# A gated cross-attention and expert block on one core: first-norm statistics moved to ScalarE, products that nobody reads, tile 1 transposed on TensorE, the first weight units split in pieces

## Chip, core and metric

The kernel runs on one core of a Trainium2 chip. The time is device microseconds of one execution. A profiled execution gives the trace; its span runs from the first to the last instruction.

## What is computed

Eight sequences of 256 tokens (2048 tokens, width 256) pass a cross-attention over 64 sets and then a block of 8 experts, of which each token takes two:

```python
def layernorm(x): return (x - mean(x)) / sqrt(var(x) + 1e-5)

# attention: token_states = layernorm(x), set_states = ctx (8, 64, 256)
q = token_states @ W_q.T + b_q
scores = (q @ desc_router.T) / 16                 # 64 sets
scores = where(set is one of the token's 4, scores, -inf)
weights = softmax(the 2 best scores)              # others 0
x = x + tanh(g_xattn) * (weights @ set_states)

# experts: xf = layernorm(x)
logits = xf @ gate_w + gate_b                     # 8 experts
top 2 logits, softmax over them; comb = gate_score * alpha
y = sum over e of comb[e] * (gelu(xf @ fc1_w[e] + fc1_b[e]) @ fc2_w[e] + fc2_b[e])
x = x + tanh(g_ffn) * y
```

## The kernel before

It is written engine by engine, with semaphores by hand; the order of the calls in each engine's block is the order of its work.

**The front, up to about 73 us.** The 16 token tiles of 128 go in four groups (g = 0 to 3) of four tiles (GT). Per group:

- `transpose_pair` (TensorE) transposes x in two pairs of tiles into banks 0 and 1, `copy_pair` (ScalarE) copies them out, `score_pair` (TensorE) multiplies by `rhs_c`, whose 73 columns are 64 projected set scores, 8 gate columns and the negative mean. `keep_gate` (ScalarE) keeps the last nine columns in `xgate`.
- `norm1` (VectorE) computes the variance of x with bn_stats and bn_aggr (four of each) and one tensor_scalar; `rsqrt` (GpSimd) makes `rs1` of it.
- `pick_sets` (VectorE) scales and masks the scores (`pick_scores`, line 982), takes the top two and marks them; `set_exp` (ScalarE) takes the exponentials; `weigh_sets` (VectorE, line 1012) makes the weights; `transpose_weights` (TensorE) and `copy_weights` (ScalarE) turn them round; `attention` (TensorE) multiplies with the sets. It needs `ctxgw` for group 0: `transpose_sets`, `copy_sets`, `set_gates` and one copy (line 822).
- `add_attention` (VectorE, from line 1020) adds the result to x; `squares` (ScalarE) and `variance2` (VectorE, line 1042) give the second variance; `route` picks two experts; `ranks` (TensorE, lines 496 to 500) counts the picks ahead of each token; `slots` (VectorE) makes places of them; `normalise` (ScalarE) and `row_low` (VectorE) write the normalised rows as two f16 parts, which SyncE stores in DRAM (`xrows`).

`projection` of the sets (line 520, read by VectorE at line 959) and the mask (lines 962 to 972) come ahead of group 0's scores. In VectorE's block `norm1(0)` stands ahead of line 959, `norm1(1)` behind the mask, `norm1(2)` and `norm1(3)` behind `pick_sets(0)` and `pick_sets(1)`.

**Into the second part, 73 to 84 us.** `token_table` sums one-hot products into a table of the tokens of each expert; from it comes `fetch_at`, with which GpSimd gathers the rows of the first four tiles (`fetch_rows`). Tile 0 is transposed by TensorE (line 589) and copied by ScalarE (line 866), tile 1 and all later ones by a transposing DMA of SyncE (line 412). The weights of 16 units (fc1 and fc2 of 8 experts, 2048 f32 columns each) lie in SBUF; a unit is split into two f16 parts by `weights_hi` (ScalarE, line 806) and `weights_lo` (VectorE, line 1297).

**The second part.** 39 tiles of 128 picks. Tile i runs fc1 in eight chunks of six products (line 615), with fc2 of the two tiles before between them (three products a chunk, line 631, 256 columns). Between stand gelu (ScalarE, line 877) and the split of its result (VectorE, lines 1432 and 1434).

## Time and profile before

| | us |
|---|---|
| median of the runs before | 307.38 (306.29 to 309.16, 3 runs) |
| span of the profiled execution | 304.3 |
| TensorE busy | 251.6 (83%) |
| VectorE busy | 213.1 (70%) |
| ScalarE busy | 177.5 (58%) |
| GpSimd busy | 147.2 (48%) |

The page's slices are 40 equal parts of the span (7.6 us each), a digit is the busy share or the granted clock in tenths. A timeline row is a start, the time to the last end, engine, line, operation and count; a bracket gives the idle time before it and what ended it. A chain row is a piece of the chain of work that ended last.

### The profile page before, as it was taken

To read this page: it belongs to the slowest core of one execution; us is meant where nothing else is said; L and a number is where in the kernel's file an instruction comes from. 1 tells how busy PE (TensorE), PEld (TensorE's weight loads), DVE (VectorE), ACT (ScalarE), POOL (GpSimd) and SP (SyncE) were. 2 spreads that over 40 slices of the span, in tenths; PEclk is the share of its full clock that TensorE was granted. 3 is DMA by queue.
4 is the path that set the end of the run, shared out by engine and by line. 5 is a ranking of instruction groups with operands and counts; after the bars stand their busy time and mean duration, and the time that the engine had idled before them with its cause. 6 is when DMAs were issued, how large, how long until landed. Compare 5 with 4: busy or idle time off the path is not lost.

```text
span 304.3 us, 9126 instructions
## 1 busy us (share of the span) xinstructions
PE 251.6 (83%) x3075; PEld 235.6 (77%) x3075; DVE 213.1 (70%) x701; ACT 177.5 (58%) x491; POOL 147.2 (48%) x122
## 2 busy tenths in 40 slices
PE   2999534241799999999999999999999999999910
PEld 2998433231689989999999999999999999989900
DVE  4899999896789778686677768677866555455500
ACT  2144878776574766856766685676666545555400
POOL 2121148994524556677545464454536355444240
PEclk9999855555599999999999999999999999999995
DMA  6999999996414444474534454455454536452320
GB/s 179 336 375 377 378 371 378 377 322 214 106 34 77 73 72 70 73 83 80 97 63 74 88 74 80 80 77 69 77 84 74 87 55 94 69 77 32 37 31 3
DMA packets 47262, 41.06 MB, mean 135 GB/s; under 512 B 23569, under 2 KB 43794, under 8 KB 47090
## 3 DMA queue, kind: packets, MB, share of 16 engines
q1 hardware_dynamic: 39088, 29.75, 33.0%
q0 software_dynamic: 7488, 10.39, 23.1%
q8 instruction: 28, 0.46, 0.6%
q10 hardware_dynamic: 642, 0.33, 0.4%
q14 instruction: 16, 0.13, 0.1%
HBM read 26.10 MB, written 9.37 MB: 117 GB/s over the span
## 4 chain that ended last, share of the span: by engine, by line
PE 60%; DVE 12%; DMA 6%; issue 3%; ACT 3%; POOL 1%; DVEq 0%; POOLq 0%; ACTq 0%
PE bank L615 30%; PE bank L631 29%; DMA out_dram<-xn,add_at 4%; DMA xs<-xrows,fetch_at 1%; DVE rows L1052 1%; DVE wreg L1061 1%; DMA xTp<-xs 1%; ACT wreg L806 1%; ACT rows L877 1%; DVE xs L1031 1%; DVE earlier L1105 1%; DVE wreg L1297 1%; DVE gmark L1095 1%; POOL out_dram L1529 1%; POOL xs L1521 1%
## 5 line engine op out<-in xcount | busy, mean ns | idle before, releaser
L615 PE MATMUL bank<-xTp,wreg 128*128 128x128 f16 x1872 | 155.3, 221 | 1.4 <-ACT xTp L866 0.7
L631 PE MATMUL bank<-wreg,rows 128*128 x936 | 150.5, 273 | 0.3 <-DVE rows L1434 0.3
L615 PEld LDWEIGHTS bank<-xTp,wreg 128*128 x1872 | 131.1, 99 | 9.6 <-issue 1.4
L877 ACT ACTIVATE rows<-bank,maskbias 128x128 f32<-128x128 f32 x312 | 88.9, 371 | 42.1 <-PE bank L615 21.6
L1529 POOL DMA_INDIRECT out_dram<-xn,add_at x39 | 66.7, 1711 | 88.1 <-DMA out_dram<-xn,add_at 48.8
L631 PEld LDWEIGHTS bank<-wreg,rows 128*128 128x128 f16 x936 | 79.1, 98 | 4.3 <-issue 0.4
L1432 DVE TENSOR_SCALAR rows<-rows 128x512 f16<-128x512 f32 x78 | 36.5, 468 | 41.6 <-ACT rows L877 41.5
L1521 POOL DMA_INDIRECT xs<-xrows,fetch_at x39 | 47.1, 1206 | 23.2 <-issue 11.3
L1434 DVE SCALAR_TENSOR_TENSOR rows<-rows 128x512 f16<-128x512 f32 x78 | 54.0, 693 | 2.7
L1297 DVE SCALAR_TENSOR_TENSOR wreg<-wreg (+1 forms) x16 | 36.7, 2292 | 13.9 <-ACT wreg L806 13.3
L885 ACT ACTIVATE xn<-xn,maskbias 128x256 f32<-128x256 f32 x39 | 20.0, 513 | 36.9 <-DVE xn L1423 36.8
L806 ACT ACTIVATE wreg<-wreg (+1 forms) x16 | 30.7, 1919 | 2.0 <-DVE wreg L1297 1.6
L1487 POOL TENSOR_TENSOR rs<-ve,neg_half 128x4 f32<-128x4 f32 x8 | 8.3, 1036 | 32.7 <-DVE ve L913 19.9
L1423 DVE SCALAR_TENSOR_TENSOR xn<-bank,xs 128x256 f32<-128x256 f32 x39 | 16.3, 418 | 7.3 <-PE bank L631 7.0
L1495 POOL TENSOR_SCALAR at_col<-iota,place_f,token 128x128 f16<-128x128 f32 x12 | 12.2, 1028 | 0.0
L498 PE MATMUL bank<-picks,before 128*128 128x32 f32 x8 | 2.5, 405 | 11.4 <-DVE earlier L1105 11.4
L498 PEld LDWEIGHTS bank<-picks,before 128*128 128x128 f32 x8 | 2.0, 316 | 11.7 <-DVE earlier L1105 7.9
L437 PE MATMUL bank<-rhs_c,xTp 128*128 128x73 f32 x64 | 10.9, 326 | 0.1
L424 PE MATMUL bank<-ident,xs 128*128 128x128 f32 x32 | 6.3, 347 | 5.5 <-DMA xs<-in_x_dram 5.5
L437 PEld LDWEIGHTS bank<-rhs_c,xTp 128*128 128x128 f32 x64 | 10.2, 242 | 0.5 <-issue 0.3
L712 ACT ACTIVATE xTp<-bank 128x512 f32<-128x512 f32 x8 | 4.7, 596 | 9.4 <-PE bank L424 9.3
L1495 POOL TENSOR_SCALAR wreg<-iota,place_f,token 128x128 f16<-128x128 f32 x8 | 8.2, 1037 | 2.7 <-DVE place_f L1153 2.7
(202 smaller groups left out, 208.0 us busy)
## 6 DMA issues: line engine op xcount, KB each, us to landing
wreg<-in_L_ffn_fc_w_dram SPq DMA_DIRECT2D x16, 1024.0 KB, 12.7
xrows<-rows SPq DMA_DIRECT2D x4, 528.0 KB, 6.4
xs<-in_x_dram SPq DMA_DIRECT2D x4, 512.0 KB, 9.3
out_dram<-xs SPq DMA_DIRECT2D x4, 512.0 KB, 9.1
xs<-in_L_ffn_fc_b_dram SPq DMA_DIRECT2D x1, 1024.0 KB, 5.7
xs<-xrows,fetch_at POOLq DMA_INDIRECT x39
out_dram<-xn,add_at POOLq DMA_INDIRECT x39
xTp<-xs SPq DMA_TRANSPOSE x38, 3.2
```

The lines of the kernel that those rows point to most:

```text
L437: mm = pe.matmul(bank[2 + g % 2][:, q * NR:(q + 1) * NR], xTp[:, j, t, k, :], rhs_c[:, k, :], start=(k == 0), stop=(k == KC - 1))
L615: mm = pe.matmul(put, w, xT[:, i % NX, x_part, k, :], start=(k == 0 and n == 0), stop=(k == KC - 1 and n == 2))
L631: mm = pe.matmul(yb, h, w, start=(c == 0 and n == 0), stop=(c == FC - 1 and n == 2))
L806: act.activation(whalf[:, bass.ds(at[1], 1), 0:UNIT].rearrange("p a n -> p (a n)"), wreg[:, bass.ds(at[0], 1), :].rearrange("p a n -> p (a ...
L877: op = act.activation(h32[i % 2][:, f * P:(f + 1) * P], bank[2 * (i % 2) + half][:, c * P:(c + 1) * P], ACT.Gelu, bias=b1cur[:, i % NX, f: ...
L885: act.activation(y_sb[:, i % 2, :], y_sb[:, i % 2, :], ACT.Copy, scale=wcur[:, i % NX:i % NX + 1]).then_inc(y_ready, 1)
L1297: v.scalar_tensor_tensor(out=whalf[:, bass.ds(at[1], 1), UNIT:2 * UNIT].rearrange("p a n -> p (a n)"), in0=wreg[:, bass.ds(at[0], 1), :].r ...
L1432: v.tensor_scalar(hhi[i % 2][:, c], h32[i % 2][:, c], H_SCALE, None, ALU.mult).then_inc(hi_done, 1)
L1434: v.scalar_tensor_tensor(out=hlo[i % 2][:, c], in0=h32[i % 2][:, c], scalar=H_SCALE, in1=hhi[i % 2][:, c], op0=ALU.mult, op1=ALU.subtract) ...
L1495: op = pool.tensor_scalar(at_col[g][:, j, :], iota[:, :], place_f[:, g, 0, j:j + 1], token[:, n:n + 1], ALU.is_equal, ALU.mult)
L1521: pool.indirect_dma_start(out=xg[:, i % NXG, :], out_offset=None, in_=xrows[:, :], in_offset=bass.IndirectOffsetOnAxis(ap=fetch_at[:, i:i ...
L1529: pool.indirect_dma_start(out=out[:, :], out_offset=bass.IndirectOffsetOnAxis(ap=add_at[:, i:i + 1], axis=0), in_=y_sb[:, i % 2, :], in_of ...
```

## The change

- `norm1` stays for group 0 alone, behind line 959. For groups 1 to 3 ScalarE's new `spread(g)` takes the squares of x minus its mean with their sum, behind `keep_gate(g)`, and VectorE's `variance1(g)` makes one tensor_scalar of the four sums.
- The order of the front changes on TensorE, ScalarE and VectorE: `score_pair(1, 1)` ahead of the transposes of group 2, these together, `transpose_weights(0)` behind the transposes of group 3, `set_exp(0)` behind the copies of group 2 and `ctxgw`, `set_exp(2)` behind `squares(0)`, `weigh_sets(1)` behind `add_attention(0)`, `weigh_sets(2)` between the halves of `add_attention(1)`.
- Products that nobody reads: UNREAD, 20 with 256 columns ahead of the first transposes; NARROW, 160 with 64 columns between `ranks(1)` and `ranks(2)`; WIDE, 36 with 128 columns between the first table product and the transposes of tile 0.
- Tile 1 is transposed as tile 0 is, behind fc1 of tile 0; the DMA takes tiles from 2 on.
- Units 0 and 1 are split in halves (`first_hi`, `first_lo`), with a semaphore of their own for each half.
- The Gelu table is loaded ahead of `column_rows(3)`.

```diff
@@ score_pair
-                if g >= 2 and j == 0:
-                    pe.wait_ge(xgate_ready, g - 1)
+                if g == 2 and j == 0:
+                    pe.wait_ge(xgate_ready, 2)
+                if g == 3 and j == 0:
+                    pe.wait_ge(scores_read, 2)
@@ tensor block
+            pe.wait_ge(ones_ready, 2)
+            for n in range(UNREAD):
+                pe.matmul(bank[3][:, 0:2 * P], ones[:, 0:P // 2].bitcast(F16), ones[:, :].bitcast(F16), start=True, stop=True)
             pe.wait_ge(pool_const, 1)
             transpose_pair(0, 0)
...
-            pe.wait_ge(mask_ready, 1)
             transpose_sets(0)
             score_pair(1, 0)
             transpose_sets(1)
+            score_pair(1, 1)
             transpose_pair(2, 0)
-            score_pair(1, 1)
+            transpose_pair(2, 1)
             pe.wait_ge(ctxT_sb, 2)
             set_gates((0, 1))
             score_pair(2, 0)
             set_gates((2, 3))
-            transpose_weights(0)
-            transpose_pair(2, 1)
-            attention(0)
             score_pair(2, 1)
             transpose_pair(3, 0)
             transpose_pair(3, 1)
+            transpose_weights(0)
+            pe.wait_ge(mask_ready, 1)
+            attention(0)
+            score_pair(3, 0)
+            score_pair(3, 1)
             transpose_weights(1)
-            score_pair(3, 0)
             attention(1)
-            score_pair(3, 1)
             transpose_weights(2)
...
             ranks(1)
+            pe.wait_ge(xT_sb, 2 * NG)
+            for n in range(NARROW):
+                pe.matmul(bank[1][:, 0:P // 2], ident_h[:, :], ident_h[:, 0:P // 2], start=True, stop=True)
             ranks(2)
...
+            for n in range(WIDE):
+                pe.matmul(bank[3][:, 0:P], ident_h[:, :], ident_h[:, :], start=True, stop=True)
+            transpose_rows(0)
...
                 tile(i, ws[i + 2], ws[i + 1], ws[i])
+                if i == 0:
+                    transpose_rows(1)
@@ scalar block
+            def spread(g):
+
+                act.wait_ge(xgate_ready, g + 1 if g >= 2 else 1)
+                for t in range(GT):
+                    n = g * GT + t
+                    act.activation(xn[:, 1, t, :], xs[:, n, :], ACT.Square, bias=xgate[:, g, t, E:G1],
+                                   accum_out=var_sum[:, n:n + 1]).then_inc(var_ready, 1)
...
             copy_sets(0)
+            copy_sets(1)
+            keep_gate(1)
+            spread(1)
             keep_gate(0)
-            set_exp(0)
-            copy_sets(1)
             copy_pair(2, 0)
+            copy_pair(2, 1)
             act.wait_ge(ctxgw_ps, 1)
             act.activation(ctxgw[:, :, 0:G1], bank[7][:, 2 * P:2 * P + NG * G1].rearrange("n (m e) -> n m e", e=G1),
                            ACT.Copy).then_inc(ctxgw_sb, 1)
-            copy_weights(0)
-            copy_pair(2, 1)
-            keep_gate(1)
-            set_exp(1)
+            set_exp(0)
...
             copy_pair(3, 0)
             copy_pair(3, 1)
+            copy_weights(0)
+            keep_gate(2)
+            spread(2)
+            set_exp(1)
             copy_weights(1)
+            keep_gate(3)
+            spread(3)
+            squares(0)
             set_exp(2)
-            squares(0)
-            keep_gate(2)
...
             column_rows(2, ((4, 5), (6, 7)))
+            act.activation(tg_gelu[:, :], gcol[:, :], ACT.Gelu)
             column_rows(3, ((0, 1), (2, 3), (4,)))
...
+            first_hi(0, 0, (first_two[0], NU))
+            first_hi(0, 1, (first_two[0], NU))
+            first_hi(1, 0, (first_two[1], first_two[0]))
...
+            copy_rows(0)
+            first_hi(1, 1, (first_two[1], first_two[0]))
...
                 gelu(i, 0)
+                if i == 0:
+                    copy_rows(1)
@@ vector block
+            def variance1(g):
                 r = slice(g * GT, (g + 1) * GT)
+                v.wait_ge(var_ready, g * GT)
+                v.tensor_scalar(ve1[:, r], var_sum[:, r], D * EPS, 1.0 / D, ALU.add, ALU.mult).then_inc(ve1_ready, 1)
...
             pick_sets(0)
-            norm1(2)
+            variance1(1)
             weigh_sets(0)
             pick_sets(1)
-            norm1(3)
+            add_attention(0, lambda: variance1(2))
             weigh_sets(1)
-            add_attention(0)
             pick_sets(2)
-            weigh_sets(2)
-            add_attention(1)
+            variance1(3)
+            add_attention(1, lambda: weigh_sets(2))
             variance2(0)
```

## Rows read from the trace of the kernel before

**Rows 1.** The page's slices, 40 of 7.6 us: TensorE's granted clock.

```profile
PEclk9999855555599999999999999999999999999995
```

**Rows 2.** Windows: length, busy us of PE, PEld, DVE, ACT, POOL, clock, DMA share, GB/s.

```profile
32.00:36.00 4.00, 2.61 (x20) 2.14 (x19) 3.66 (x18) 3.75 (x17) 1.01 (x1) 0.99 1.09 373
80.00:84.00 4.00, 4.00 (x40) 3.84 (x37) 3.04 (x5) 1.78 (x5) 0.95 (x1) 0.54 0.69 135
```

**Rows 3.** Timeline of TensorE, 0 to 110 us: start, us to last end, line, operation.

```profile
14.14 1.82 PE L437 MATMUL bank<-rhs_c,xTp 128*128 128x73 f32 x8
...
19.40 0.60 PE L424 MATMUL bank<-ident,xs 128*128 128x128 f32 x4
19.84 1.01 PE L437 MATMUL bank<-rhs_c,xTp 128*128 128x73 f32 x8
20.69 1.00 PE L451 MATMUL bank<-rhs_c,xn 128*128 128x9 f32 x8
...
56.48 0.64 PE L498 MATMUL bank<-picks,before 128*128 128x32 f32 x2 [7.38 <-DVE earlier L1105]
...
72.82 0.19 PE L585 MATMUL bank<-is_col,tokens_at 128*128 128x4 f16 x1 [0.37 <-ACT tokens_at L860]
77.62 0.59 PE L589 MATMUL bank<-ident_h,xs 128*128 128x128 f16 x4 [4.61 <-DMA xs<-xrows,fetch_at]
78.89 5.13 PE L615 MATMUL bank<-xTp,wreg 128*128 128x128 f16 x48 [0.69 <-ACT xTp L866]
```

**Rows 4.** TensorE's waits, 84 to 304 us.

```profile
PE bank L615 <- DMA xTp<-xs: 0.3, 1, 0.3
```

**Rows 5.** Chain of waits, 0 to 130 us: start, length, what.

```profile
75.98 4.24 DMA xs<-xrows,fetch_at
80.26 4.05 DMA xTp<-xs
84.35 1.85 PE bank L615 x30
```

**Rows 6.** Timeline of VectorE, 0 to 60 us.

```profile
1.03 0.17 DVE L916 MEMSET ones<- 128x128 f32 x1
...
11.37 0.16 DVE L962 CAST itok_f<-itok 128x8 f32<-128x8 int32 x1
...
13.60 1.41 DVE L907 BATCH_NORM_STATS2 stats<-xs 128x6 f32<-128x256 f32 x4
...
16.00 0.86 DVE L982 SCALAR_TENSOR_TENSOR pick_buf<-bank,rs,maskbias 128x64 f32<-128x64 f32 x4 [0.37 <-PE bank L437]
...
18.60 1.39 DVE L907 BATCH_NORM_STATS2 stats<-xs 128x6 f32<-128x256 f32 x4
...
20.52 0.43 DVE L1012 SCALAR_TENSOR_TENSOR pick_buf<-pick_buf 128x256 f32<-128x256 f32 x1
...
26.30 0.17 DVE L1020 RECIPROCAL den<-bank 128x4 f32<-128x4 f32 x1
...
34.07 0.16 DVE L1042 TENSOR_SCALAR ve<-sq_sum 128x4 f32<-128x4 f32 x1
...
57.58 0.19 DVE L1120 TENSOR_TENSOR pick_slots<-picks,bank 128x32 f32<-128x32 f32 x1 [0.86 <-PE bank L500]
```

**Rows 7.** Timeline of ScalarE, 0 to 115 us.

```profile
18.28 1.05 ACT L730 ACTIVATE pick_buf<-pick_buf,neg_top 128x64 f32<-128x64 f32 x4
...
31.27 0.49 ACT L750 ACTIVATE xn<-xs,ugate 128x256 f32<-128x256 f32 x1
...
75.11 1.28 ACT L864 ACT_TABLE_LOAD   x1
...
78.24 0.60 ACT L866 ACTIVATE xTp<-bank 128x512 f16<-128x512 f32 x1 [1.63 <-PE bank L589]
```

**Rows 8.** DMA issues that start in 2.3 to 2.6 us: KB, us to landing.

```profile
xs<-in_x_dram SPq DMA_DIRECT2D x1, 512.0 KB, 8.4
```

**Rows 9.** TensorE's weight loads by form, 36 to 83.5 us: busy us, mean ns.

```profile
L585 PEld LDWEIGHTS bank<-is_col,tokens_at 128*128 128x128 f16 x1 | 0.1, 105 | 0.6 <-ACT tokens_at L860 0.6
```

More of the change, by code:

```diff
@@ L340, in flamingo_block @@
         added = sem("added")
-        FIRST_UNITS = 2
+        UNREAD = 20
+        FIRST_BY_PE = 2
+        NARROW, WIDE = 160, 36
         units_of_tile = {1: (2,), 3: (3,)}
@@ L405, in _ @@
             sp.dma_start(b2_all[:, :, :], fc2_b.rearrange("(a e) d -> a e d", a=1).to_broadcast([P, E, D])).then_inc(b2_in, 16)
-            for i in range(1, TILES):
+            for i in range(FIRST_BY_PE, TILES):
                 if i >= NX:
@@ L801, in unit_regions, with first_hi @@
                 return region_now[0], put
+            def first_hi(k, half, at):
+                if k == 1 and half == 0:
+                    act.wait_ge(half_lo, 1)
+                c = slice(half * (UNIT // 2), (half + 1) * (UNIT // 2))
+                act.activation(whalf[:, bass.ds(at[1], 1), c].rearrange("p a n -> p (a n)"),
+                               wreg[:, bass.ds(at[0], 1), c].rearrange("p a n -> p (a n)"),
+                               ACT.Copy, scale=W_SCALE).then_inc(half_hi, 1)
             def weights_hi(k, at):
-                if k >= 1:
-                    act.wait_ge(w_lo, k)
+                if k == 2:
+                    act.wait_ge(half_lo, 4)
+                else:
+                    act.wait_ge(w_lo, k - 2)
                 act.activation(whalf[:, bass.ds(at[1], 1), 0:UNIT].rearrange("p a n -> p (a n)"),
@@ L840, in _ @@
             normalise(0)
-            keep_gate(3)
             copy_weights(3)
@@ L960, in _ @@
                             ALU.mult).then_inc(rhs_ready, 1)
+            norm1()
             v.wait_ge(itok_in, 16)
@@ L1026, in add_attention @@
                 for j in range(2):
+                    if j == 1 and between:
+                        between()
                     v.wait_ge(attn_ps, 2 * g + j + 1)
```

104 lines of the change are left out of this document (65 added, 39 removed).

## Prediction

> **What bounds the kernel now.** I read the slices of the page first. TensorE's granted clock is at its full level (2.4 GHz) in the first 36 us, at half (1.2 GHz) up to about 84 us, and full to the end [rows 1, 2]. The durations say more than the record for the start: the eight score products of a pair took 1.82 us at 14.14 us and 1.01 us at 19.84 us [rows 3]. So the array worked at half pace up to about 18.6 us, whatever the granted clock reads there.
>
> Then the chain of waits and TensorE's waits. From 84.35 us, where tile 1's fc1 starts, TensorE's waits to the end are three of 0.3 us, one of which is shown [rows 4]. That stretch is TensorE's own work at full clock, and the change adds to it only four small products. So the change is worth what it moves the start of tile 1's fc1, the 84.35 us. Before it the chain is, from the end: the transposing DMA of tile 1's rows (4.05 us), the gather of those rows (4.24 us behind the second gather's issue), and ahead of that almost all VectorE, which waits 0.86 us for the rank products at 57.58 us and for little else [rows 5, 6]. Two questions decide: when does VectorE reach variance2(0), at 34.07 us now [rows 6], and how long is it from the first gather to tile 1.
>
> **Statistics on ScalarE.** What leaves VectorE: norm1 of groups 1 to 3. One takes 1.92 us of it: norm1(2) starts at 18.60 and gives way at 20.52 [rows 6]; three are 5.8 us. In their place come three tensor_scalars of 0.1 us. ScalarE gets twelve squares with their sums; four of its present squares (0.49 us each, issued end to end) take 2.0 us with the read of the sum [rows 7]. These need the group's mean, which comes from the scores: spread(1) can't start before score_pair(1,1). So work goes off VectorE, but VectorE gets new waits. I walk the path with the present durations, first with TensorE at full pace from about 6.0 us (whether it is, is the next part).
>
> - proj and its copy are at about 9.1 us; norm1(0), now behind it, ends at 11.0, the mask work (11.37 to 13.60 now, 2.2 us) at 13.2. pick_sets(0) starts at 13.2 instead of 16.00 [rows 6]: 2.8 us ahead.
> - TensorE gets x of group 1 at 2.4 + 8.4 = 10.8 us [rows 8]. From there: transposes 0.44 us, scores 0.85 (by the starts from 19.40 to 20.69 [rows 3]; 0.6 and 1.0 with the end of the last) and the two transpose_sets: score_pair(1,1) ends at 15.3. keep_gate(1) and spread(1) end at 17.7. VectorE finished pick_sets(0) at 15.8 and waits 1.9 us in variance1(1).
> - weigh_sets(0) needs set_exp(0), which on ScalarE is now behind spread(1), both copies of group 2 and the copy of ctxgw. That copy needs set_gates(2,3), those stand behind score_pair(2,0), and that needs copy_pair(2,0), which is over at 18.3: scores to 19.3, gates to 20.2, ctxgw 0.2, exp 1.05 [rows 7]: 21.4. VectorE waits 3.6 us. weigh_sets(0) is at 21.4 against 20.52 [rows 6].
> - pick_sets(1) ends at 24.4, attention(0) at 24.75 (transposes and copy_weights(0) lie behind the copies of group 3). add_attention(0) starts at 24.75 against 26.30: 1.55 ahead, as norm1(2) and norm1(3) are gone.
> - weigh_sets(1) is now behind it, at 27.1; pick_sets(2) waits 0.3 us for rs1(2). On ScalarE: copy_weights(1) 28.0, spread(3) to 30.5, squares(0) to 32.4, and only then set_exp(2), to 33.5. add_attention(1) starts at 30.6 (wait 0.15), and its weigh_sets(2) waits 1.4 us for set_exp(2). variance2(0) is at 34.65.
>
> Sum against 34.07: -2.8 (start) -3.85 (two blocks) +0.3 (three small ones) +7.7 (new waits, with some 0.3 of rounding) -0.7 (two waits of now that go) = +0.6 us. The 5.8 us are given back as waits. From there VectorE's order is as before and is carried with +0.6. norm1(1) had cover from nothing; the stall's price is what stands queued behind the waiting variance1: weigh_sets and pick_sets, and for them TensorE's transpose_weights.
>
> **UNREAD.** 20 products of 256 columns. 128 columns take 107 ns at half clock (48 in 5.13 us [rows 3]), so 213 ns each, 4.3 us from the memset of ones at 1.2 us [rows 6] to 5.5 us, where the first transposes wait anyway for x: no cost beyond 0.1. In tile 0 the clock rose 4.8 us into dense products: they start at 78.89, and 80 to 84 us has a mean of 0.54, that is full for the last 0.3 us [rows 2, 3]. Dense 4.3 us and the transposes behind them are as long, so I take the rise at about 6 us. It is worth much: with half pace up to 18.6 us the same walk gives score_pair(1,1) at 20.4 instead of 15.3.
>
> **NARROW.** 160 products of 64 columns between ranks(1) and ranks(2). TensorE is free for 7.4 us there, up to 56.48 us [rows 3] (both shift alike). Cost of one: bounded below by columns (53 ns at half clock, 28 at full: 30 products of 128 took 1.85 us with the end of the last [rows 5]), above by the 107 and 56 ns of the pair of load and product with 128 columns. At the lower bound: 90 in the 4.8 us to the rise, 70 in 2.0, over after 6.8 us: it fits. Then ranks(2) runs at full clock and VectorE's wait of 0.86 us for it [rows 6] shrinks by 0.5 (half of the 1.1 us from 56.48 to 57.58). At 53 then 56 ns: 8.7 us, 1.3 late, net +0.8. A lone f16 load took 105 ns even at half clock, with its fixed part [rows 9], and a fixed part there must be, so I stand near the lower bound and take -0.4.
>
> The Trainium skill (TensorE: Matmul & The Clock Gate, LDWEIGHTS) puts a load of 128 columns at 107 ns. By it NARROW would be 160 x 107 = 17 us, ranks(2) 9.7 us late, and the sum some 10 us worse. At full clock the trace speaks against it: the pair of load and product there has 56 ns.
>
> **WIDE, transposes of tile 1, units in pieces, Gelu table.** WIDE starts behind the product at 72.82 and takes 36 x 107 = 3.9 us, to 76.8; rows 0 come at 77.62 [rows 3]: free. With it fc1 of tile 0 runs at full clock: 48 x 56 ns = 2.7 us instead of 5.13, and the transposes ahead of it take 0.3 us less. So fc1(0) runs from 78.6 to 81.3; tile 1's rows lie in SBUF since 80.26 [rows 5]; four products 0.4, copy_rows(1) 0.6 [rows 7] (gelu(0,0) ahead of it on ScalarE is done at 81.3), tile 1 at 82.4 instead of 84.35: -1.95. With half clock instead it would be 78.9 + 5.1 + 1.1 = 85.1, +0.75. The pieces let the second unit's first half through earlier; x, not the weights, is last for fc1(0), and fc2(0) comes 1.3 us into tile 1, so nothing. The moved Gelu table load (1.28 us [rows 7]) falls into ScalarE's wait for slots(3); uncovered it would delay the last token table by up to 1.3.
>
> **Sum.** +0.6 -0.4 -1.95 = -1.8 us on the profiled span of 304.3, 302.5. The median before, 307.4, lies 3.1 above that span, and I carry it: 305.6.
>
> **Rivals.**
> - *Loads set NARROW's pace.* For: f32 products took the same time with 9 columns (1.00 us for eight) as with 73 (1.01) [rows 3], so there the load paces. With f16 at the upper bounds: 45 products in 4.8 us, 115 x 56 ns = 6.4, together 11.2, ranks(2) 3.8 us late less 0.5: 3.3 instead of -0.4. 309.3, the other side. It decides from a mean of 46 ns a product on, where NARROW fills its gap. The rule of the skill above is this rival without a rise. 0.18.
> - *The clock falls again in the front.* Products are sparse while x of group 1 is awaited; in 32 to 36 us TensorE was busy 2.61 of 4 us and the clock fell at the end [rows 2]. About 2 us of the front's products doubled: 307.6. 0.13.
> - *The front stays at half pace.* UNREAD does nothing: score_pair(1,1) 5.1 us later, 310.7. Slower than before from 1.8 us of delay on. Against: 4.3 us of full-width products. 0.08.
> - *Tile 0 stays at half clock* (a gap of 0.8 us behind WIDE): 305.6 + 2.7 = 308.3. 0.06.
> - *The new waits are half what I make them.* For: seven links of my walk are on the one chain over score_pair, spread and exp, and an early one pays in all. 3 to 4 us less: 302. 0.13.
>
> The forecast itself has 0.42, with 304.3 to 307.2 as its own range.
>
> **How the numbers follow.** 1% is 3.1 us, about what a measurement of this kernel tells from no change. Faster by more: the last rival and the forecast's tail, with some room for links that I made too long, 0.24. Slower: the front at half pace, NARROW without a rise, sums of two rivals, 0.18. Within: 0.58. The range goes from 303.2 (part of the last rival) to 309.6 (NARROW at its upper bound).
>
> **What would show it.** Right: the transposes at 5.5 us pace at 107 ns or soon do; VectorE waits about 2 us at variance1(1), 3.6 at weigh_sets(0), 1.4 at weigh_sets(2); variance2(0) at 34 to 35.5 us; ranks(2) at once behind picks; fc1(0) in about 2.7 us, tile 1 at 82 to 83.5 us; no new wait behind it. Wrong: ranks(2) waits for NARROW's end; transposes of group 1 still at 213 ns; a second table load on ScalarE; tile 1 waiting for its gather.

## The result, and the profile after

| | before | after |
|---|---|---|
| median, us (lowest to highest, executions) | 307.14 (306.29 to 309.16, 4) | 310.57 (307.96 to 313.35, 4) |
| ratio, 95% interval | | 1.0098 (1.0054 to 1.0143) |
| span of the profiled execution | 304.3 | 306.2 |
| TensorE busy | 251.6 | 262.5 |
| VectorE busy | 213.1 | 207.6 |
| ScalarE busy | 177.5 | 184.2 |

The change makes the kernel 1.0% slower, where 305.6 (303.2 to 309.6) was forecast. The profiled execution is the lowest of the four (307.96 us; its span is 306.2, and time less span is 1.75 to 1.8 us in each). The other three are 2.3 to 5.4 us longer, and their granted clock, as a mean over the execution, is lower (0.883 to 0.890, against 0.903). So the trace below shows the loss at its smallest: +1.9 us of span, where the medians differ by 3.4.

A ratio here leaves out executions more than 1.5% above the lowest of their kernel; where one kernel scatters that far it comes out lower than the quotient of the medians, and then I read both.

TensorE's granted clock, 40 slices of 7.7 us, then windows of the front and of tile 0 (columns as in [rows 2]):

```profile
PEclk9968555855799999999999999999999999999975
```

```profile
12.00:16.00 4.00, 4.00 (x40) 4.00 (x38) 3.76 (x21) 2.65 (x7) 1.14 (x1) 1.00 1.05 350
16.00:20.00 4.00, 2.62 (x17) 2.55 (x16) 0.44 (x4) 2.35 (x9) 1.02 (x1) 0.78 1.07 376
20.00:24.00 4.00, 4.00 (x20) 4.00 (x20) 1.30 (x6) 1.24 (x6) 0.00 (x0) 0.50 1.07 371
24.00:28.00 4.00, 3.31 (x27) 2.93 (x25) 1.83 (x16) 3.64 (x13) 0.00 (x0) 0.87 1.05 382
80.00:84.00 4.00, 2.42 (x40) 2.26 (x41) 3.62 (x10) 2.51 (x5) 2.37 (x3) 1.00 0.35 101
```

Against [rows 1, 2]: before, the clock was full to 36 us. Now it is at half already from about 18 to 25 us, and again from 32 us on. In return it is full in the later half of NARROW's stretch, and in all of 80 to 84 us. TensorE's timeline shows what the first fall did:

```profile
14.80 1.04 PE L430 MATMUL bank<-ident,xs 128*128 128x128 f32 x8
15.68 0.96 PE L459 MATMUL bank<-rhs_c,xn 128*128 128x9 f32 x8
18.02 1.75 PE L445 MATMUL bank<-rhs_c,xTp 128*128 128x73 f32 x8 [1.38 <-ACT xTp L746]
19.57 1.80 PE L459 MATMUL bank<-rhs_c,xn 128*128 128x9 f32 x8
21.22 1.96 PE L445 MATMUL bank<-rhs_c,xTp 128*128 128x73 f32 x8
22.98 1.91 PE L430 MATMUL bank<-ident,xs 128*128 128x128 f32 x8
...
52.62 6.26 PE L591 MATMUL bank<-ident_h 128*128 128x64 f16 x160
60.19 0.41 PE L506 MATMUL bank<-picks,before 128*128 128x32 f32 x2 [1.31 <-DVE earlier L1177]
...
76.09 0.19 PE L600 MATMUL bank<-is_col,tokens_at 128*128 128x4 f16 x1 [0.37 <-ACT tokens_at L920]
76.14 3.84 PE L602 MATMUL bank<-ident_h 128*128 128x128 f16 x36
80.80 0.40 PE L607 MATMUL bank<-ident_h,xs 128*128 128x128 f16 x4 [0.82 <-DMA xs<-xrows,fetch_at]
81.97 2.86 PE L643 MATMUL bank<-xTp,wreg 128*128 128x128 f16 x48 [0.78 <-ACT xTp L929]
84.67 0.39 PE L607 MATMUL bank<-ident_h,xs 128*128 128x128 f16 x4
```

Read it from the top. Up to 16.64 us a group of eight takes 0.96 to 1.04 us, the full pace. Then TensorE is idle for 1.38 us, until ScalarE has copied group 2. The four groups behind the gap take 1.75 to 1.96 us each, where [rows 3] had 1.00 and 1.01. The first two lie ahead of the copy of `ctxgw` and so of group 0's exponentials, all four ahead of group 0's attention (ScalarE, then VectorE):

```profile
17.30 1.06 ACT L746 ACTIVATE xTp<-bank 128x512 f32<-128x512 f32 x2
21.41 0.20 ACT L878 ACTIVATE ctxgw<-bank 128x36 f32<-128x36 f32 x1 [3.05 <-PE bank L459]
21.50 1.05 ACT L776 ACTIVATE pick_buf<-pick_buf,neg_top 128x64 f32<-128x64 f32 x4
```

```profile
13.58 0.86 DVE L1052 SCALAR_TENSOR_TENSOR pick_buf<-bank,rs,maskbias 128x64 f32<-128x64 f32 x4
...
17.34 0.17 DVE L984 TENSOR_SCALAR ve<-var_sum 128x4 f32<-128x4 f32 x1 [1.07 <-ACT xn L768]
22.66 0.43 DVE L1082 SCALAR_TENSOR_TENSOR pick_buf<-pick_buf 128x256 f32<-128x256 f32 x1 [5.15 <-ACT pick_buf L776]
...
27.75 0.18 DVE L1090 RECIPROCAL den<-bank 128x4 f32<-128x4 f32 x1 [2.06 <-PE bank L482]
...
37.77 0.16 DVE L1114 TENSOR_SCALAR ve<-sq_sum 128x4 f32<-128x4 f32 x1
...
60.86 0.19 DVE L1192 TENSOR_TENSOR pick_slots<-picks,bank 128x32 f32<-128x32 f32 x1 [0.43 <-PE bank L508]
```

VectorE begins group 0's picks 2.4 us earlier than in [rows 6] (13.58 for 16.00), then waits 5.15 us for the exponentials and 2.06 for group 0's attention. variance2(0) is at 37.77 for 34.07: +3.7. The second fall, at 32 us, adds nothing to it: from 27.75 to 37.77 are 10.02 us, as in the runs below in which the clock fell at 28.6 us (e2) or stayed full to 36 us (e7). From variance2(0) the order of before carries it on, with a wait of 0.43 for 0.86 at the rank products. The chain of waits into the second part (answering [rows 5]) has lost the transposing DMA:

```profile
77.43 3.33 DMA xs<-xrows,fetch_at
80.80 0.41 PE bank L607 x4
81.24 0.61 ACT xTp L929
81.97 2.86 PE bank L643 x48
85.10 0.60 ACT xTp L929
85.75 1.85 PE bank L643 x30
```

Tile 1 starts at 85.75 for 84.35. From the first table product (76.09, before 72.82) to it are 9.66 us, before 11.53: -1.87. So: +3.7 (front) -0.43 (NARROW) -1.87 (tile 1) = +1.4, measured 85.75 - 84.35 = 1.40. Behind it 220.45 us for 219.95 make the rest of the span's +1.9; TensorE's one wait for VectorE's rows there grew from 0.28 to 0.61 us.

### The profile page after: what moved, and what is told of

It is laid out like the page before. It is cut to its first block, busy times and chain, and to the rows that moved or that the text cites. A ratio compares the mean times of both kernels' runs of the same rounds, so it can differ in the third digit from the quotient of the medians.

```text
span 306.2 us, 9575 instructions
## 1 busy us (share of the span) xinstructions
PE 262.5 (86%) x3295; PEld 244.3 (80%) x3295; DVE 207.6 (68%) x679; ACT 184.2 (60%) x518; POOL 151.3 (49%) x122
## 4 chain that ended last, share of the span: by engine, by line
PE 60%; DVE 5%; DMA 5%; ACT 3%; issue 3%; POOL 1%; DVEq 0%; POOLq 0%; ACTq 0%
PE bank L643 31%; PE bank L663 28%; DMA out_dram<-xn,add_at 4%; ACT wreg L862 1%; DMA xs<-xrows,fetch_at 1%; ACT rows L942 1%; DVE wreg L1380 1%; POOL out_dram L1613 1%; DVE rows L1124 0%; DVE wreg L1133 0%; DVE rows L1515 0%; ACT xTp L929 0%; ACT xn L950 0%; PE bank L584 0%; DVE xn L1133 0%
## 5 line engine op out<-in xcount | busy, mean ns | idle before, releaser
L643 PE MATMUL bank<-xTp,wreg 128*128 128x128 f16 x1872 | 153.0, 219 | 1.6 <-ACT xTp L929 1.5
L643 PEld LDWEIGHTS bank<-xTp,wreg 128*128 x1872 | 128.7, 98 | 10.1 <-ACT xTp L929 1.8
L1605 POOL DMA_INDIRECT xs<-xrows,fetch_at x39 | 50.6, 1298 | 22.9 <-issue 11.3
L1380 DVE SCALAR_TENSOR_TENSOR wreg<-wreg x14 | 32.1, 2292 | 12.1 <-ACT wreg L862 11.3
L862 ACT ACTIVATE wreg<-wreg x14 | 26.9, 1921 | 1.9 <-DVE wreg L1380 1.9
L445 PE MATMUL bank<-rhs_c,xTp 128*128 128x73 f32 x64 | 9.9, 308 | 1.4 <-ACT xTp L746 1.4
L445 PEld LDWEIGHTS bank<-rhs_c,xTp 128*128 128x128 f32 x64 | 9.2, 222 | 1.5 <-ACT xgate L760 1.4
L482 PEld LDWEIGHTS bank<-ctxgw,wT 64*128 64x128 f32 x32 | 6.8, 276 | 3.3 <-ACT wT L783 1.9
L806 ACT ACTIVATE xn<-xs,shift,rs 128x256 f32<-128x256 f32 x16 | 8.3, 587 | 1.4 <-DVE shift L1120 1.4
L491 PE MATMUL bank<-ctx_sb,wT 64*128 64x256 f32 x32 | 8.6, 597 | 0.0
```

Source lines behind the costliest of these rows:

```text
L445: mm = pe.matmul(bank[2 + g % 2][:, q * NR:(q + 1) * NR], xTp[:, j, t, k, :], rhs_c[:, k, :], start=(k == 0), stop=(k == KC - 1))
L643: mm = pe.matmul(put, w, xT[:, i % NX, x_part, k, :], start=(k == 0 and n == 0), stop=(k == KC - 1 and n == 2))
L862: act.activation(whalf[:, bass.ds(at[1], 1), 0:UNIT].rearrange("p a n -> p (a n)"), wreg[:, bass.ds(at[0], 1), :].rearrange("p a n -> p (a ...
L1380: v.scalar_tensor_tensor(out=whalf[:, bass.ds(at[1], 1), UNIT:2 * UNIT].rearrange("p a n -> p (a n)"), in0=wreg[:, bass.ds(at[0], 1), :].r ...
L1605: pool.indirect_dma_start(out=xg[:, i % NXG, :], out_offset=None, in_=xrows[:, :], in_offset=bass.IndirectOffsetOnAxis(ap=fetch_at[:, i:i ...
```

## Experiments

"Old front" is the front of the kernel before: its order, norm1 for every group on VectorE. "Filled" adds f16 products of 128 columns that nobody reads. Medians are over all executions (number in brackets), before is that of the same chip; clock is TensorE's granted clock, a mean over the executions; v2 is the start of variance2(0) in the profiled execution.

| kernel | median, us | before | ratio (interval) | clock | v2, us |
|---|---|---|---|---|---|
| the change | 310.57 (4) | 307.14 | 1.010 (1.005, 1.014) | 0.892 | 37.77 |
| e1 old front, with UNREAD and the rest | 305.10 (6) | 306.99 | 0.987 (0.983, 0.991) | 0.907 | 37.84 |
| e2 change, first gap filled | 307.39 (6) | 306.99 | 1.000 (0.995, 1.004) | 0.907 | 34.95 |
| e3 change, exponentials first | 311.66 (6) | 306.99 | 1.016 (1.013, 1.020) | 0.895 | 40.68 |
| e4 change without UNREAD | 314.90 (4) | 306.99 | 1.025 (1.019, 1.030) | 0.899 | 43.84 |
| e5 as e1, without UNREAD | 304.71 (12) | 306.96 | 0.994 (0.991, 0.996) | 0.923 | 36.05 |
| e6 old front, only tile 1 and pieces | 306.64 (12) | 306.96 | 1.001 (0.998, 1.005) | 0.904 | 33.83 |
| e7 change, all gaps filled, WIDE 48 | 304.98 (12) | 306.96 | 0.995 (0.992, 0.998) | 0.925 | 34.75 |
| e8 old front, filled, WIDE 48 | 305.33 (12) | 306.96 | 0.994 (0.989, 0.998) | 0.915 | 33.44 |
| e9 the change's front alone | 310.81 (6) | 306.71 | 1.013 (1.008, 1.019) | 0.872 | 38.91 |
| e10 as e7, NARROW 0 | 306.62 (12) | 306.71 | 0.997 (0.994, 1.001) | 0.913 | 38.20 |
| e11 as e7, WIDE 0 | 308.24 (12) | 306.71 | 1.004 (1.001, 1.007) | 0.915 | 36.77 |
| e12 as e8, early gaps filled too | 304.89 (6) | 306.71 | 0.989 (0.983, 0.995) | 0.922 | 34.45 |
| e13 change, spread(1) behind copies | 305.58 (13) | 306.42 | 0.994 (0.989, 0.998) | 0.904 | 36.62 |
| e14 change, statistics on VectorE | 308.09 (12) | 306.42 | 0.998 (0.993, 1.003) | 0.900 | 35.17 |
| e15 as e13, filled, WIDE 48 | 305.46 (12) | 306.42 | 0.997 (0.993, 1.000) | 0.924 | 38.14 |
| e16 as e14, filled, WIDE 48 | 305.56 (12) | 306.42 | 0.996 (0.993, 0.999) | 0.925 | 35.02 |

### Which part loses: e1, e9, e6, e5

e1: all of the change but its front; UNREAD stays.

```diff
@@ against the kernel before; order of the front, norm1, set_exp, copies: unchanged
+            pe.wait_ge(ones_ready, 2)
+            for n in range(UNREAD):
...
@@ NARROW, WIDE, transpose_rows(1), first_hi, first_lo: as in the change
```

> The front of before (norm1 of all groups on VectorE, its old order) with everything else of the change: UNREAD, NARROW, WIDE, transposes of tile 1 on TensorE, units in pieces, Gelu table ahead. Theory A (the new front is the loss, the rest gains): variance2(0) at 34.0 us or a little earlier, fetch_at at about 72.6, tile 1 at 82.0 us, span about 302, some 2.4 us below before, ratio 0.992. Rival B (the rest costs: the products or the new order of the units): as slow as the changed kernel or slower than before, ratio 1.00 to 1.01.

The gain is there: median 305.10 for 306.99. The executions lie between 301.94 and 307.80, three below 303.1 and three above 307.1, so the ratio is that of the lower three. The profiled one is of the upper three, and it shows the same fall of the clock in the old front, behind a gap as well:

```profile
18.20 1.06 PE L455 MATMUL bank<-rhs_c,xn 128*128 128x9 f32 x8 [1.55 <-ACT xn L747]
19.12 1.55 PE L441 MATMUL bank<-rhs_c,xTp 128*128 128x73 f32 x8
20.46 1.80 PE L455 MATMUL bank<-rhs_c,xn 128*128 128x9 f32 x8
```

e9: the front alone, NARROW = WIDE = 0, tile 1 by the DMA. UNREAD, the halves of units 0 and 1 and the early Gelu table stay.

```diff
-        FIRST_BY_PE = 2
-        NARROW, WIDE = 160, 36
+        FIRST_BY_PE = 1
+        NARROW, WIDE = 0, 0
...
-                if i == 0:
-                    transpose_rows(1)
```

> Of the change, the front alone: its order, the statistics of groups 1 to 3 on ScalarE, UNREAD = 20, the halves of units 0 and 1 and the early Gelu table; NARROW = WIDE = 0 and tile 1 by the transposing DMA as in the kernel before. The counterpart of the run with the old front and the rest of the change (ratio 0.987). Theory A (front loses 3 to 5 us by half pace in it, the later part gains 2): group 0's second variance at 37.5 to 38.5, the first places of picks at 61.3, ratio 1.014 (1.010 to 1.019), span of the profiled execution 307.5 to 310. Rival (the two parts do not add up: the later part's products are what spoils the next executions' front, by heat or power): front alone at full clock, second variance at 34.7, ratio 1.000 to 1.004.

1.013, as theory A had it, v2 at 38.91. By medians the front alone is 1.0134 and the rest alone (e1) 0.9938; the product, 1.007, is near the change's 1.011. So the loss is in the front; the 0.4% between 1.007 and 1.011 is no more than these medians scatter.

e6: of the rest, only tile 1 on TensorE, units in pieces, Gelu table.

```diff
@@ against e1
-        UNREAD = 20
-        NARROW, WIDE = 160, 36
+        UNREAD = 0
+        NARROW, WIDE = 0, 0
```

> Front as in the kernel before and no products that nobody reads anywhere (UNREAD = NARROW = WIDE = 0); only the transposes of tile 1 on TensorE, units 0 and 1 in halves, and the early Gelu table. Theory (forecast's mechanism): WIDE is what gives the gain; without it fc1 of tile 0 takes about 5.1 us at half clock as in the kernel before (4.9 or more), and tile 1 starts where the load's tile did or a little later: ratio 1.002 (0.999 to 1.005), tile 1 at 11.0 to 12.0 us behind fetch_at. Rival: taking the tile off the transposing DMA (whose load landed last before) gains by itself: ratio 0.994 to 0.996, tile 1 at 9.5 to 10.5 us behind fetch_at.

```profile
77.30 0.61 PE L603 MATMUL bank<-ident_h,xs 128*128 128x128 f16 x4 [4.53 <-DMA xs<-xrows,fetch_at]
78.60 4.90 PE L639 MATMUL bank<-xTp,wreg 128*128 128x128 f16 x48 [0.69 <-ACT xTp L910]
```

Without WIDE fc1 of tile 0 takes 4.90 us, and tile 1 starts at 84.41 us, 11.82 behind the table product (before 11.53): no gain.

e5: as e1, `UNREAD = 0`.

> Front as in the kernel before (order, norm1 for all groups), UNREAD = 0; NARROW, WIDE, tile 1 on TensorE, units in pieces and the early Gelu table as in the change. Left out beside the change: the 20 products UNREAD. With UNREAD in this old front TensorE ran out of work at 16.65 us (1.55 us for the set transposes' copies) and its clock fell at 19.7. Theory A (the clock falls where a TensorE that is fast from the start runs dry): without UNREAD the first transposes and score products go at half pace up to about 15.5 us as in the kernel before, TensorE has no gap ahead of the set gates, the clock stays full to about 36 us, group 0's second variance starts at 34.1 (+-0.3), fetch_at at 72.6, tile 1 at 82.1, span 302.0, ratio 0.992 (0.989 to 0.995), and its runs differ less among themselves (under 3 us) than those of the front with UNREAD (5.9 us). Rival (the later part's change shifts the front's clock, or the fall is chance): the front falls to half in some executions, group 0's second variance at 37 to 38 and ratio 0.997 or more. Rival 2 (UNREAD pays by itself even in the old front, since the last x transposes come 0.5 to 2 us earlier): ratio above 0.987 by the worth of UNREAD, so 0.990 to 0.995 as well, but with a second variance later than with UNREAD in an execution at full clock.

0.994, with 303.5 to 307.6 us over twelve executions. Theory A's ratio holds, but not its picture: the profiled execution had the clock at half from 24.5 to about 31 us and v2 at 36.05. With the old front UNREAD gives nothing by the medians (305.10 and 304.71) and the executions scatter more with it (standard deviation 2.7 us over six, against 1.2 over twelve).

### Why the front loses: e2, e3, e4

e2: 24 filling products ahead of `score_pair(2, 0)`.

```diff
             set_gates((0, 1))
+            pe.wait_ge(ident_ready, 1)
+            for n in range(24):
+                pe.matmul(bank[4][:, 0:P], ident_h[:, :], ident_h[:, :], start=True, stop=True)
             score_pair(2, 0)
```

> The changed kernel with 24 more unread f16 products of 128 columns in bank 4, between set_gates(0,1) and score_pair(2,0), where TensorE stood idle from 16.6 to 18.0 us and its clock fell. Theory A (the clock's fall in the front made the difference to my walk): clock stays full over 16 to 25 us, set_exp(0) ends at about 21.4 instead of 22.5, add_attention(0) starts at 24.8 to 25.5 instead of 27.75, variance2(0) at about 34.7 instead of 37.77, span 303 to 304. Rival B (the waits by order are the loss, the clock only follows): under 1 us gained. Rival C: the clock falls in the next gap instead, 1 to 2 us gained.

```profile
21.50 0.42 DVE L1085 SCALAR_TENSOR_TENSOR pick_buf<-pick_buf 128x256 f32<-128x256 f32 x1 [3.73 <-ACT pick_buf L779]
24.93 0.18 DVE L1093 RECIPROCAL den<-bank 128x4 f32<-128x4 f32 x1 [0.42 <-PE bank L482]
...
34.95 0.16 DVE L1117 TENSOR_SCALAR ve<-sq_sum 128x4 f32<-128x4 f32 x1
```

Work that gives nothing makes the front 2.8 us shorter (34.95 for 37.77). The four groups that took 6.67 us in the change (18.02 to 24.69) take 3.69 here. The forecast's walk had 21.4, a wait of 3.6, 24.75 and 34.65. But behind WIDE the clock fell in this execution, tile 1 came at 85.15, and the median is only that of before:

```profile
79.80 4.44 PE L646 MATMUL bank<-xTp,wreg 128*128 128x128 f16 x48 [0.77 <-ACT xTp L932]
```

e3: `set_exp(0)` ahead of `spread(1)` on ScalarE, so that VectorE's longest wait goes.

```diff
             keep_gate(1)
+            set_exp(0)
             spread(1)
...
                            ACT.Copy).then_inc(ctxgw_sb, 1)
-            set_exp(0)
```

> The changed kernel with set_exp(0) moved from behind the copy of ctxgw to between keep_gate(1) and spread(1). Theory B (the loss is the place of set_exp(0)): weigh_sets(0) at about 18.5 instead of 22.66 us, pick_sets(1) 4 us earlier; add_attention(0) still needs ctxgw and copy_weights(0) and so gains at most 1 to 2 us; spread(1) is 1 us later and with it score_pair(2,0). Theory A (the path is TensorE's and ScalarE's chain, VectorE's wait is only its shadow): add_attention(0) within 1 us of 27.75, span within 1.5 us of the changed kernel's.

```profile
19.01 0.43 DVE L1082 SCALAR_TENSOR_TENSOR pick_buf<-pick_buf 128x256 f32<-128x256 f32 x1
20.42 0.86 DVE L1052 SCALAR_TENSOR_TENSOR pick_buf<-bank,rs,maskbias 128x64 f32<-128x64 f32 x4 [0.98 <-POOL rs L1571]
29.96 0.18 DVE L1090 RECIPROCAL den<-bank 128x4 f32<-128x4 f32 x1 [6.86 <-PE bank L482]
```

The 5.15 us in front of weigh_sets(0) are gone, and 6.86 stand one step later; v2 is 2.9 us later, the ratio 1.016. VectorE's wait only mirrored TensorE's chain, which the move made longer: TensorE's gap grew to 2.42 us, and behind it the clock was at half to past variance2(0).

e4: `UNREAD = 0` in the change.

> The changed kernel without UNREAD. If UNREAD is what brings the front to full pace: transposes and scores at half pace up to 16 us or later, score_pair(1,1) at 20.4 instead of 15.0 us, variance2(0) 3 to 5 us later than 37.77, span 308 to 311. If the clock's fall at 18 us takes all of it back anyway: variance2(0) within 1 us of 37.77.

score_pair(1, 1) starts at 20.04 us (13.95 with UNREAD), v2 is 6.1 us later, 1.025. The walk at half pace had it end at 20.4 (measured 21.0, 15.0 with UNREAD). In this front UNREAD is worth 4.3 us by the medians.

### Is the forecast's sum right at full clock: e7, e10, e11

e7: the front's three gaps filled, WIDE 48.

```diff
@@ e2's 24 products, and:
-        NARROW, WIDE = 160, 36
+        NARROW, WIDE = 160, 48
...
             score_pair(3, 1)
+            for n in range(14):
+                pe.matmul(bank[0][:, 0:P], ident_h[:, :], ident_h[:, :], start=True, stop=True)
             transpose_weights(1)
             attention(1)
+            for n in range(36):
+                pe.matmul(bank[0][:, 0:P], ident_h[:, :], ident_h[:, :], start=True, stop=True)
             transpose_weights(2)
```

> The change with more products that nobody reads, f16, 128 columns: 24 ahead of group 2's first score products, 14 ahead of the transposes of group 1's weights, 36 ahead of those of group 2's, and WIDE raised from 36 to 48. Theory A: the clock is full from 6 us to about 33, group 0's second variance starts at 34.7 (34.5 to 35.2), fetch_at 73.3, WIDE now ends behind the landing of tile 0's rows so that tile 0 runs at full clock in every execution (fc1 2.9 us), tile 1 at 9.4 to 9.7 us behind fetch_at; span 303.0, ratio 0.992 (0.989 to 0.996), and less than 3 us between its runs. Rival: the products in the later gaps delay the weights' transposes (they stand in TensorE's queue where ScalarE's copies or VectorE's weights come late by chance), group 0's second variance at 35.5 or later, ratio 1.000 as with the first gap alone.

```profile
34.75 0.16 DVE L1121 TENSOR_SCALAR ve<-sq_sum 128x4 f32<-128x4 f32 x1
...
57.83 0.19 DVE L1199 TENSOR_TENSOR pick_slots<-picks,bank 128x32 f32<-128x32 f32 x1 [0.43 <-PE bank L508]
```

v2 is 34.75 (the walk: 34.65), and the median is 1.98 us below before, where the forecast's sum was -1.8. The trace does not bear the sum out that closely: tile 1 starts 0.96 us earlier than before (83.39), made of +0.68 (front), -0.43 (NARROW) and -1.29 (tile 1 is 10.24 us behind the table product, 9.66 in the change: the gathered rows came 0.6 us later). So the front and NARROW are as forecast, and that the median agrees so well is in part luck. The twelve executions have a standard deviation of 0.9 us; e2's six have 3.0. Two things differ from e2, the two later fillings and WIDE 48, and in the traces it is WIDE that tells: v2 is only 0.2 us earlier than in e2, but tile 0 runs at full clock and tile 1 starts 1.8 us earlier:

```profile
79.64 2.84 PE L650 MATMUL bank<-xTp,wreg 128*128 128x128 f16 x48 [0.77 <-ACT xTp L936]
```

So WIDE 36 was itself too short to count on. In the eight traces with WIDE 36 fc1 of tile 0 takes 2.84 to 2.94 us in three (the change, e1, e5) and 4.44 to 5.30 us in five (e2, e3, e4, e13, e14); in the six with WIDE 48 it takes 2.84 to 2.86. No run changes WIDE to 48 alone, so how much of e7's gain over e2 in the median is the fillings is not shown.

e10: the same, NARROW = 0.

> The change with every gap of the front filled and WIDE 48 (ratio 0.995, span 303.7), but NARROW = 0. Forecast's step: NARROW shortens VectorE's wait for the second table rank from 0.86 to 0.43 us and nothing else, so that wait is 0.86 again, fetch_at is 0.4 us later, ratio 0.9965 (0.993 to 1.000). Rival (NARROW is worth more, since the clock is full behind it for the table products too): ratio 0.999 or more; rival (its 160 products cost nothing and give nothing): 0.995.

```profile
60.66 0.60 PE L506 MATMUL bank<-picks,before 128*128 128x32 f32 x2 [7.42 <-DVE earlier L1184]
```

VectorE's wait behind it is 0.87 us again for 0.43: the forecast's term of 0.4. The ratio can't tell it from zero. By the medians, each less its own before, e10 is 1.9 us slower than e7, more than that term; its trace has the clock at half from about 10.5 to 17.3 us, long ahead of NARROW's place, with v2 at 38.20. Whether NARROW has a part in that difference is not shown.

e11: the same, WIDE = 0.

> The change with every gap of the front filled (ratio 0.995, span 303.7), but WIDE = 0. Forecast's step: without WIDE tile 0 runs at half clock (fc1 4.9 to 5.1 us in place of 2.84), tile 1 starts 11.2 to 12.0 us behind fetch_at in place of 9.8, ratio 1.001 (0.998 to 1.005). Rival (NARROW's clock lasts until tile 0, or tile 0's own transposes raise it): fc1 at 2.9 us, tile 1 within 10.2 us, ratio 0.995.

```profile
79.82 0.61 PE L614 MATMUL bank<-ident_h,xs 128*128 128x128 f16 x4 [4.44 <-DMA xs<-xrows,fetch_at]
81.11 5.22 PE L650 MATMUL bank<-xTp,wreg 128*128 128x128 f16 x48 [0.69 <-ACT xTp L936]
```

fc1 of tile 0 takes 5.22 for 2.84 us; tile 1 starts 12.06 us behind the table product, in e7 10.24. WIDE is worth 0.9% by the ratios (1.004 for 0.995), or 2.8 us, and 3.5 us by the medians; the forecast had 2.7 us between tile 0 at full and at half clock.

### Which part of the front: e13 to e16

e13: the squares of group 1 behind the copies of group 2.

```diff
             keep_gate(1)
-            spread(1)
             keep_gate(0)
             copy_pair(2, 0)
             copy_pair(2, 1)
+            spread(1)
```

> The change with spread(1) (four squares of 0.42 us on ScalarE) moved behind the copies of group 2, so that score_pair(2, 0) no longer waits for it. Theory A (place of spread(1)): TensorE's idle ahead of score_pair(2, 0) shrinks from 1.38 us to 0.3 or less, the clock falls in the front later or not, group 0's exponentials are no later, the second variance of group 0 at 34.5 to 36.5 in place of 37.8, ratio 0.996 (0.992 to 1.002), TensorE's granted clock over an execution 0.905 to 0.915 in place of 0.883 to 0.903. Theory B (the statistics cost ScalarE's time wherever they stand): the set exponentials come as late, the second variance at 37 or later, ratio 1.007 to 1.013. Rival (the order, not the statistics): a gap of over 1 us opens elsewhere ahead of the set gates, ratio 1.007 to 1.013.

One line moved takes the change from 1.010 to 0.994; the intervals do not touch. By the medians, each by its own before, it is 1.011 and 0.997. The profiled execution is one of the longest (span 309.1), and is worth reading for that:

```profile
16.90 1.09 PE L445 MATMUL bank<-rhs_c,xTp 128*128 128x73 f32 x8
17.83 1.00 PE L459 MATMUL bank<-rhs_c,xn 128*128 128x9 f32 x8
18.69 1.19 PE L445 MATMUL bank<-rhs_c,xTp 128*128 128x73 f32 x8
19.68 1.91 PE L430 MATMUL bank<-ident,xs 128*128 128x128 f32 x8
```

```profile
20.13 0.42 DVE L1082 SCALAR_TENSOR_TENSOR pick_buf<-pick_buf 128x256 f32<-128x256 f32 x1 [1.04 <-ACT pick_buf L776]
...
36.62 0.16 DVE L1114 TENSOR_SCALAR ve<-sq_sum 128x4 f32<-128x4 f32 x1
```

The gap is gone, and the clock fell all the same, at about 19.5 us, with TensorE busy without a break from 12 us on. So the gap is not needed for a fall. What the move does surely is shorten the chain: weigh_sets(0) at 20.13 for 22.66, and a smaller part of it lies behind the fall. The thirteen executions run from 302.57 to 310.89 us, longer where their mean clock is lower (correlation -0.94). The front is not all that made the profiled one long: of its 4.8 us of span over before, 1.9 lie ahead of tile 1's start (86.27, with fc1 of tile 0 at 4.47 us), and 2.9 behind it.

e14: the statistics back on VectorE, order as in the change; `spread` goes.

```diff
             pick_sets(0)
-            variance1(1)
+            norm1(1)
+            norm1(2)
             weigh_sets(0)
             pick_sets(1)
-            add_attention(0, lambda: variance1(2))
+            norm1(3)
+            add_attention(0)
...
-            variance1(3)
```

> The change with the statistics of groups 1 to 3 back on VectorE as bn_stats and bn_aggr (about 1.9 us a group), groups 1 and 2 ahead of weigh_sets(0), where VectorE waited 5.15 us, group 3 ahead of add_attention(0), where it waited 2.06; no spread on ScalarE; order and the rest as in the change. Theory A: no idle ahead of score_pair(2, 0), exponentials 1.5 us earlier, the second variance of group 0 at 33.5 to 35.5, ratio 0.992 (0.987 to 0.998). Theory B gives the same here. Rival (the order makes the loss): the second variance at 37 or later, ratio 1.005 to 1.013. Rival (VectorE becomes the bound): the second variance at 36 with VectorE without a wait over 0.5 us between 15 and 34 us, ratio 1.000.

0.998, v2 at 35.17. The ratios of e13 and e14 overlap, and by the medians e14 is the slower by 2.5 us. So it is the place of spread(1) that costs, and not that ScalarE makes the statistics; taking them back to VectorE is no better. Its front is not what makes e14 slower than e13, as far as two traces tell: v2 is 1.4 us earlier than in e13, but tile 0 ran at half clock:

```profile
80.37 5.30 PE L643 MATMUL bank<-xTp,wreg 128*128 128x128 f16 x48 [0.69 <-ACT xTp L926]
```

e15 is e13, and e16 is e14, with e7's three fillings and WIDE 48.

> spread(1) behind the copies of group 2 and all gaps filled as before (24, 14 and 36 products, WIDE 48). Against the same fillings with spread(1) in its place (0.995, second variance at 34.75): theory A, the clock was full there already, so only the copies' 1.4 us can come out, of which the filler of 1.5 us takes as much again; second variance at 34.3 to 34.8, ratio 0.994 (0.990 to 0.998). Rival (the front is bound by ScalarE's chain even at full clock): second variance at 33.3, ratio 0.990.

> Statistics back on VectorE in the new order, all gaps filled, WIDE 48: candidate for a kernel better than both. Theory A: full clock and the shorter chain on ScalarE, second variance of group 0 at 33.0 to 34.0, span 301.5 to 302.5, ratio 0.988 (0.984 to 0.992). Rival (order at fault): ratio 0.995 or more, as with the statistics on ScalarE and the same fillings.

e15 0.997, e16 0.996, beside 0.995 for e7: with the gaps filled and WIDE 48 the three can't be told apart. e15 missed its v2 (38.14), as the clock was at half in its profiled execution from about 11 to 17 us. e16's hope of 0.988 was wrong, and so was its v2 (35.02 for 33.0 to 34.0): the clock fell in its trace at 29 us, behind a gap of 1.55 us, and TensorE then kept VectorE waiting 1.59 us ahead of add_attention(1). What the place of the statistics is worth with the clock held to the end of the front, these two do not show.

### A kernel better than both: e8, e12

Both are e1 with fillings; e8 has 24 products ahead of the wait for `ctxT_sb` and 16 ahead of `transpose_weights(2)`, WIDE 48, and the copy at line 959 ahead of norm1(0). e12 adds:

```diff
-        UNREAD = 20
+        UNREAD = 23
@@ projection
             mm.then_inc(descT_ps, 1)
+            for n in range(4):
+                pe.matmul(bank[3][:, 0:2 * P], ones[:, 0:P // 2].bitcast(F16), ones[:, :].bitcast(F16), start=True, stop=True)
             pe.wait_ge(descT_sb, 1)
```

> Candidate for a kernel better than both: front in the order of the kernel before with norm1 for all groups, but VectorE's copy of the projection ahead of norm1(0); UNREAD 20; 24 f16 products of 128 columns that nobody reads ahead of the set gates (where TensorE ran dry for 1.55 us) and 16 ahead of the transposes of group 2's weights; WIDE 48; the rest as the change. Theory A: the clock stays full from 6 us to about 33, group 0's second variance at 33.0 to 34.0, fetch_at at 71.8 to 72.6, tile 1 9.4 to 9.7 us behind it, span 300.5 to 301.5, ratio 0.986 (0.982 to 0.990), with runs within 3 us. Rival: VectorE is the bound of this front whatever TensorE's pace; the second variance stays at 34.1, ratio 0.990 to 0.993.

> The old front with UNREAD and the filled gaps, WIDE 48 (ratio 0.994; its executions fell into two bunches, six with spans of 300.9 to 302.4 and six with 304.8 to 305.9 us, and the profiled one of the lower bunch had the clock at half from 10.8 to 14 us), now with UNREAD 23 and 4 more products of that kind ahead of the projection, so that TensorE has neither of its two early gaps (0.4 us at 5.8 and at 8.5). Theory A: the upper bunch is a fall of the clock in the front that starts at a gap; with the gaps closed nearly all executions lie in the lower bunch, median 303.5, ratio 0.988 (0.984 to 0.992). Rival: the f32 products of this stretch let the clock fall whether there are gaps or not; two bunches as before, ratio 0.992 to 0.996.

Both are faster than before. Ratios 0.994 and 0.989, medians 1.6 and 1.8 us below it. e12's theory falls, since two bunches remain (300.9 to 303.7 us of span, and 305.6 and 306.0). The profiled execution is of the lower bunch, and even there the clock fell at about 23 us inside attention(0), with no gap right ahead of it; what makes the upper bunch was seen in no trace. By the medians e1, e5, e7, e8 and e12 are level (304.7 to 305.3): 0.5 to 0.7% better than before, and none of them is shown to be the best.

## Why the prediction was wrong

1. **The step that failed** is the premise that the walk rests on, "with TensorE at full pace from about 6.0 us", held to the end of the front. The rise itself came, as the part on UNREAD said: the eight transposes of the first group, from 5.95 us, take 1.07 us. But the clock fell at 18 us and was back at 25, and add_attention(0) started at 27.75 us for 24.75: +3.0 us of the +3.1 by which the front missed (+3.7 for +0.6). e2 shows it, where the clock was kept and that start is at 24.93. The mechanism stood among the rivals, "The clock falls again in the front", with 2 us and a chance of 0.13. Its place was wrong (I looked at the wait for group 1). Its price was too low, since four groups of f32 products in a row lie on the chain. Its chance was too low as well: of the 14 traces taken with UNREAD, with either front, only e7's has the clock full from 10 to 30 us.
2. **The gap stood in the walk.** By its own terms TensorE was through with the gates of the first sets by about 17 us, and copy_pair(2,0) was over at 18.3. I priced that idle time as delay and not for the clock, though [rows 2] show a window in which TensorE was idle for 1.4 of 4 us and the clock fell at its end. In the change the clock fell behind just such a gap. That the gap is the cause is not shown, since in e13 it fell without one.
3. **The rest of the walk held.** Picks at 13.6 (13.2), score_pair(1,1) over at 15.0 (15.3); in e2 weigh_sets(0) at 21.5 (21.4), add_attention(0) at 24.9 (24.75), v2 at 34.95; in e7 34.75 (34.65). The wait at variance1(1), 1.07 for 1.9, was made too long; the one at weigh_sets(2), 0.72 for 1.4, is 1.37 in e7, where the clock is full.
4. **NARROW** was right, for the right reason: 160 products in 6.26 us (6.8 forecast), the wait 0.43 for 0.86, and e10 gives it back. Its mean was 39 ns over the change of clock, so the rival from 46 ns on falls. The rule of the Trainium skill (TensorE: Matmul & The Clock Gate, LDWEIGHTS) puts a load of 128 columns at 107 ns. The trace disagrees: here 160 such loads went by in 6.26 us.
5. **WIDE and tile 1** came out right in the change's trace: -1.87 for -1.95, fc1 of tile 0 2.86 us for 2.7; e6 and e11 put the gain down to WIDE's clock. That it came out so was in part luck. "Tile 0 stays at half clock" had a chance of 0.06, and with WIDE 36 it is there, in whole or for the most part, in five of eight traces (4.44 to 5.30 us).
6. **One execution for a median.** The sum was laid on one trace and carried to the median with 3.1 us. Of the 5.0 us between 305.6 and 310.57, 3.1 are the front, 0.5 the second part, 0.1 NARROW and tile 1, and 1.3 this carry: the median of the change lies 4.4 us above its profiled span. Over 103 executions before has 304.6 to 310.8 us (standard deviation 1.4), and its time falls as its clock rises (correlation -0.61). The change widened this: its own four span 5.4 us, e2's six 8.1. What its longer executions lose beyond the +1.9 of the trace was seen in no trace of it, and stays open. Other kernels' traces show two likely forms: e9, whose clock stayed at half from 19.8 us through the whole front (v2 at 38.91), and the five with tile 0 at half clock, 1.6 to 2.4 us each.

## What to carry to other kernels

A walk along the chain can be right in each link and still give the wrong sign, if the pace of the engine that it runs over is taken as given: list where that engine will stand idle after the change, and price a fall of its clock at each place by what stands behind it. A fall can come without idle time too, as in e13. Put work that others wait for (here two copies) ahead of work that only makes room (the squares), even when the engine has time for both. A stretch whose clock changes from one execution to the next must be judged by many executions, and by a trace of a long one as well as of a short one.
